# Weight tiles times q and k in f16 parts, exponentials read from PSUM, four counted groups per query block

## The reference, cut to what matters

```python
xr = jnp.einsum('nd,rdf->rnf', x, W)          # graph attention, per edge type r
qi = xr[etype, dst] @ q;  kj = xr[etype, src] @ k
alpha = leaky_relu(qi + kj, 0.2)              # softmax of alpha over the edges of each dst
out = segment_sum(a * xr[etype, src], dst) + b
...
qf, kf = phi(q), phi(k)                       # linear attention, phi(x) = x+1 if x>0 else exp(x)
y = (qf @ (kf^T v)) / max(qf . sum(kf), 1e-6);  y @ W_out + b_out
```

## Time and profile before

| | |
|---|---|
| runs, us | 1745.96, 1751.33, 1743.84 (median 1745.96) |
| profiled execution, its own time | 1746.55 us |
| its span, first to last instruction | 1744.8 us |
| PE, PEld busy | 1631.8 us (94%), 1191.5 us (68%) |
| DVE, ACT, POOL busy | 1308.5 us (75%), 774.8 us (44%), 138.1 us (8%) |
| mean granted TensorE clock | 0.962 |
| DMA | 183.3 MB, 105 GB/s over the span |

### The profile page before, as it was taken

One profiled execution on the slowest core, in us unless ns is written; L12 is line 12 of the kernel. 1 busy time (PEld: TensorE's weight loads), 2 busy tenths in 40 slices (PEclk: granted clock), 3 DMA queues, 4 the chain that ended last, 5 costly groups with the idle time before them and its releaser, 6 DMA issues.

```text
span 1744.8 us, 34402 instructions
## 1 busy us (share of the span) xinstructions
PE 1631.8 (94%) x10547; PEld 1191.5 (68%) x10548; DVE 1308.5 (75%) x2631; ACT 774.8 (44%) x1021; POOL 138.1 (8%) x245
## 2 busy tenths in 40 slices
PE   4999999999999999879999999989899799999987
PEld 3566667778755666479999999986555455555544
DVE  8699876786649999258899898972764377777785
ACT  4331112331234565168888898862212133333342
POOL 2000000000000000000000000000000033333340
PEclk9999998987999999989999999989999999999998
DMA  5111123224467664541004132132664631011122
GB/s 192 38 57 61 60 59 116 78 88 143 156 186 221 197 201 141 152 126 58 30 30 133 46 111 73 40 99 85 196 182 138 199 139 54 1 53 54 60 62 89
DMA packets 130308, 183.30 MB, mean 105 GB/s; under 512 B 14934, under 2 KB 100088, under 8 KB 130220
## 3 DMA queue, kind: packets, MB, share of 16 engines
q1 hardware_dynamic: 130220, 182.17, 33.5%
HBM read 121.33 MB, written 60.81 MB: 104 GB/s over the span
## 4 chain that ended last, share of the span: by engine, by line
PE 80%; DVE 8%; issue 4%; DMA 3%; ACT 2%; DVEq 1%; POOL 1%; SPq 1%; ACTq 0%; POOLq 0%
PE ps L2041 22%; PE ps L1992 12%; PE ps L2099 7%; PE ps L2098 7%; PE ps L1819 6%; PE ps L1806 4%; PE ps L1807 4%; PE ps L1808 4%; PE ps L1901 3%; PE ps L1880 3%; PE ps L2110 1%; PE ps L1977 1%; DVE oh_q L1340 1%; DMA xr_d<-ev 1%; PE ps L1862 1%
## 5 line engine op out<-in xcount | busy, mean ns | idle before, releaser
L2041 PE MATMUL ps<-xrh,pf 128*128 (+1 forms) x2400 | 399.4, 329 | 11.3 <-DVE pf L1617 11.3
L2041 PEld LDWEIGHTS ps<-xrh,pf 128*128 128x128 f32 x2400 | 393.1, 191 | 17.7 <-issue 15.3
L1806 PE MATMUL ps<-w_hi,xt_hi 128*128 128x384 f16 x600 | 198.8, 331 | 23.1 <-DVE ev L1663 14.7
L1613 DVE SCALAR_TENSOR_TENSOR vb<-vb,tb 128x1260 f32<-128x1260 f32 x120 | 172.8, 1465 | 53.1 <-ACT vb L1114 52.2
L1340 DVE TENSOR_SCALAR oh_q<-pat,codeT,neg_w 125x630 f16<-125x630 uint16 x420 | 186.4, 444 | 34.3 <-PE ps L1819 23.5
L2098 PE MATMUL ps<-x,ph 128*128 (+1 forms) x600 | 196.6, 328 | 15.8 <-POOL pl L916 9.9
L1617 DVE SCALAR_TENSOR_TENSOR pf<-vb,CT 128x1260 f32<-128x1260 f32 x120 | 175.7, 1467 | 34.9 <-PE ps L2041 34.9
L1807 PE MATMUL ps<-w_lo,xt_hi 128*128 128x384 f16 x600 | 198.9, 332 | 0.0
L1808 PE MATMUL ps<-w_hi,xt_lo 128*128 128x384 f16 x600 | 198.7, 331 | 0.0
L2099 PE MATMUL ps<-x,ph 128*128 (+1 forms) x600 | 197.8, 330 | 0.0
L1114 ACT ACTIVATE vb<-qbc,kcol 128x1260 f32<-128x1260 f32 x120 | 161.0, 1345 | 39.1 <-DVE pf L1617 37.7
(11 more groups left out here) (235 smaller groups left out, 2454.9 us busy)
## 6 DMA issues: line engine op xcount, KB each, us to landing
qbc<-tq_d SPq DMA_DIRECT2D x12, 1260.0 KB, 6.4
wst<-in_L_gnn_W SPq DMA_DIRECT2D x60, 192.0 KB, 3.2
xr_d<-ev SPq DMA_DIRECT2D x60, 192.0 KB, 2.0
xrh<-xr_d SPq DMA_DIRECT2D x4, 2880.0 KB, 14.9
x_d<-ev SPq DMA_DIRECT2D x60, 192.0 KB, 2.3
mb_d<-mb SPq DMA_DIRECT2D x30, 310.1 KB
mb<-mb_d SPq DMA_DIRECT2D x30, 310.1 KB
x<-x_d SPq DMA_DIRECT2D x2, 3840.0 KB, 19.3
```

The costliest lines, as they stand in the source:

```text
L1613: dve.scalar_tensor_tensor(vb[j][:, :], vb[j][:, :], 2.0, tb[j][:, :], ALU.min, ALU.max).then_inc(v_step, 1)
L1806: pe.matmul(ps[:, bank, 0:CW], a_hi, hi[:, k, :], start=(k == 0), stop=False)
L2041: mm = pe.matmul(out[b], pf[j][:, b * DB:b * DB + P], x, start=(first and b % 2 == 0), stop=False, skip_group_check=True)
```

## The change

- `wq_tile`: ACT writes f16 hi parts of each weight tile (times 16, `wt_high`), DVE the lo parts (`wt_low`), POOL those of q and k, and PE does 18 f16 matmuls for a tile in place of 6 in f32. A tile stands ahead of each step of a block, from the third step of the first block on; tiles 34 and 35 stand in the attention rows.
- A query block has four windows (`QW = 4`), and the attention rows keep three.
- ACT reads the query products straight from PSUM (Relu with the bias folded in), and DVE makes `QF` from PSUM in one instruction; the banks are now freed by that (`q_out`; `q_free` is gone). DVE's lo part of chunk 5 moves behind the first block.
- `bsum` and `acc_d<-X` are gone: the two biases enter the output projection as a matmul of three bf16 rows per product (20 of them), and its input rows are read from `x`.
- Layer 1's `node_columns` moves into the attention rows (blocks 5 to 9), `wqk_hi` and `wqk_lo` into blocks 2 and 3.
- In keys and values DVE reads the window's registers ahead of its waits.
- Layer 2: hi and lo parts of chunks 2 to 5 are made in thirds between the pairs of the chunk before; the first weights of the aggregation start before the last pair.

```diff
+            def wt_high(t):
+
+                act.wait_ge(wt_in[t % 6], 16 * (t // 6 + 1))
+                if t >= 3:
+                    act.wait_ge(wt_used, t - 2)
+                act.activation(wt_hi[t % 3][:, :], wt[t % 6][:, :], ACT.Copy, scale=SPLIT).then_inc(wt_hi_done, 1)
+
+            act.wait_ge(bq_done, 1)
             for c in range(2):
                 for fb in range(3):
-                    wa = W_Q + 3 * (3 * c + fb)
-                    late_out(wa)
-                    late_out(wa + 1)
+                    q = 3 * c + fb
+                    wa = W_Q + QW * q
+                    for k in range(K6):
+                        if k in (2, 4, 5)[:QW - 1]:
+                            late_out(wa + (2, 4, 5).index(k))
+                        wt_high(6 * q + k)
                     for g in range(NRG):
-                        n = (3 * c + fb) * NRG + g
-                        act.wait_ge(q_free, n + 5)
-                        act.wait_ge(q_out, n + 1)
-                        act.activation(q_m[g % 2][:, :], q_t[g % 2][:, :], ACT.Relu, scale=-1.0).then_inc(q_mm, 1)
+                        n = q * NRG + g
+                        act.wait_ge(q_done, n + 1)
+                        if n >= NRG:
+                            act.wait_ge(q_out, n - NRG + 1)
+                        act.activation(q_m[g][:, :], ps[:, g, 0:RG], ACT.Relu, bias=nbq[:, q:q + 1], scale=-1.0).then_inc(q_mm, 1)
                         act.wait_ge(q_mm, n + 1)
-                        act.activation(q_m[g % 2][:, :], q_m[g % 2][:, :], ACT.Exp, scale=-1.0).then_inc(q_ee, 1)
-                    late_out(wa + 2)
+                        act.activation(q_m[g][:, :], q_m[g][:, :], ACT.Exp, scale=-1.0).then_inc(q_ee, 1)
+                    late_out(wa + QW - 1)
                 w_hi_part(C_O + c)
...
+                if 1 <= m < 2 * R - 1:
+                    with act.Fori(0, 3) as ii:
+                        x2_hi(m, ii)
+                        act.wait_ge(w_in[c % 2], 16 * loads_to(c))
+                        weights_free(act, c - 2)
+                        act.activation(w_hi[c % 2][:, ds(2 * ii, 2), :], wst[c % 2][:, ds(2 * ii, 2), :], ACT.Copy).then_inc(w_hi_done, 1)
...
-                        count_part(W_K + 2 * ii + j + 1)
+                        one_hots(W_K + 2 * ii + j + 1, *of_w)
...
+            def wt_low(t, k):
+
+                dve.wait_ge(wt_hi_done, t + 1)
+                dve.scalar_tensor_tensor(wt_lo[k % 3][:, :], wt[k][:, :], SPLIT, wt_hi[k % 3][:, :], ALU.mult, ALU.subtract).then_inc(wt_lo_done, 1)
+
+            def query_block(q):
+
+                wa = W_Q + QW * q
+                for k in range(K6):
+                    wt_low(6 * q + k, k)
+                    if k in (1, 3, 4)[:QW - 1]:
+                        count_part(wa + (1, 3, 4).index(k) + 1)
+                for g in range(NRG):
+                    n = q * NRG + g
+                    dve.wait_ge(q_ee, n + 1)
+                    dve.scalar_tensor_tensor(sub(QF, q)[:, g * RG:(g + 1) * RG], ps[:, g, 0:RG], sub(bq1, q), q_m[g][:, :],
+                                             ALU.add, ALU.max).then_inc(q_out, 1)
+                count_part(wa + QW)
+
             count_part(W_Q)
             dve.wait_ge(ct_out[0], 16 * (3 * NB // 2 + 2) + 16)
             dve.wait_ge(ct_out[1], 16 * (3 * NB // 2 + 1) + 16)
-            for c in range(2):
-                if c == 1:
-                    dve.wait_ge(xb_done, 1)
-                with dve.Fori(0, 3) as fb:
-                    for u in range(2):
-                        count_part(W_Q + 3 * (3 * c + fb) + u + 1)
-                    for g in range(NRG):
-                        n = (3 * c + fb) * NRG + g
-                        dve.wait_ge(q_done, n + 1)
-                        dve.wait_ge(q_out, n + 1)
-                        dve.tensor_scalar(q_t[g % 2][:, :], ps[:, g, 0:RG], sub(bq_col, 3 * c + fb), None, ALU.add).then_inc(q_free, 1)
-                        if g % 2:
-                            for g2 in (g - 1, g):
-                                n2 = (3 * c + fb) * NRG + g2
-                                dve.wait_ge(q_ee, n2 + 1)
-                                dve.scalar_tensor_tensor(sub(QF, 3 * c + fb)[:, g2 * RG:(g2 + 1) * RG], q_t[g2 % 2][:, :], 0.0, q_m[g2 % 2][:, :],
-                                                         ALU.max, ALU.add).then_inc(q_out, 1)
-                    count_part(W_Q + 3 * (3 * c + fb) + 3)
-                    if c == 1:
-                        for u in range(3):
-                            dve.tensor_tensor(sub(X, 3 * fb + u), sub(X, 3 * fb + u), bsum[:, :], ALU.add).then_inc(xb_done, 1)
-            dve.tensor_tensor(X[:, NB - 1, :], X[:, NB - 1, :], bsum[:, :], ALU.add).then_inc(xb_done, 1)
+            dve.wait_ge(bq_done, 1)
+            query_block(0)
+            w_lo_part(5)
+            with dve.Fori(1, K6) as q:
+                query_block(q)
...
+                        x2_lo(m, ii)
+                        if 1 <= m < 2 * R - 1 and i0 == 1:
+                            low_piece(c, ii - 1)
...
+                    cols = slice(k * P, (k + 1) * P)
+                    pe.matmul(o, hi[:, cols], q_hi, start=(t % (WT_TILES // 2) == 0 and k == 0), stop=False, skip_group_check=True)
+                    pe.matmul(o, hi[:, cols], q_lo, start=False, stop=False, skip_group_check=True)
+                    last = pe.matmul(o, lo[:, cols], q_hi, start=False, stop=(nb == K6 - 1), skip_group_check=True)
...
-                    wa = W_Q + 3 * (3 * c + fb)
-                    of_w = [window(pe, wa + u)[1:] for u in range(3)]
+                    wa = W_Q + QW * (3 * c + fb)
+                    of_w = [window(pe, wa + u)[1:] for u in range(QW)]
                     for k in range(K6):
-                        if k in (2, 4):
-                            count_window(wa + k // 2 - 1, 6, *of_w[k // 2 - 1])
+                        if k in (2, 4, 5)[:QW - 1]:
+                            u = (2, 4, 5).index(k)
+                            count_window(wa + u, 6, *of_w[u])
+                        t = 6 * (3 * c + fb) + k - 2
+                        if t == 0:
+                            pe.wait_ge(kvd_done, 2)
+                            pe.wait_ge(qk_ready, 70)
+                        if t >= 0:
+                            wq_tile(t)
                         w_h, w_l = w_hi[cc % 2][:, k, fb * P:(fb + 1) * P], w_lo[cc % 2][:, k, fb * P:(fb + 1) * P]
                         for step, (w, t) in enumerate(((w_h, xt_hi), (w_h, xt_lo), (w_l, xt_hi))):
                             for g in range(NRG):
                                 n = (3 * c + fb) * NRG + g
-                                if k == 0 and step == 0:
-                                    pe.wait_ge(q_free, n + 1)
+                                if k == 0 and step == 0 and n >= NRG:
+                                    pe.wait_ge(q_out, n - NRG + 1)
                                 last = pe.matmul(ps[:, g, 0:RG], w, t[:, k, g * RG:(g + 1) * RG], start=(k == 0 and step == 0),
                                                  stop=(k == K6 - 1 and step == 2))
                                 if k == K6 - 1 and step == 2:
                                     last.then_inc(q_done, 1)
-                    if c == 0 and fb == 0:
-                        pe.wait_ge(kvd_done, 2)
-                        pe.wait_ge(qkn_in, 64)
-                    for t in range(3 * (3 * c + fb), 3 * (3 * c + fb) + 3):
-                        wq_tile(t)
-                    count_window(wa + 2, 6, *of_w[2])
-
-            of_w = window(pe, W_A - 1)[1:]
-            for t in range(WT_TILES // 2, WT_TILES // 2 + 3):
-                wq_tile(t)
-            count_window(W_A - 1, 6, *of_w)
...
+                if i < 2:
+                    wq_tile(WT_TILES - 2 + i)
+                if i >= NB // 2:
+                    if i == NB // 2:
+                        pe.wait_ge(wqk_step, 4)
+                    node_columns(wqk_hi, wqk_lo, 2 * R * H, 2 * i - NB, 2 * i - NB + 2)
...
+                    if c < C_X and q % PM == 0:
+                        pe.matmul(ps[:, 6 + n % 2, 0:CW], one3[:, :], orow[:, (c - C_O) * CW:(c - C_O + 1) * CW], start=True, stop=False)
...
-            pe.wait_ge(wqk_step, 4)
-            node_columns(wqk_hi, wqk_lo, 2 * R * H)
```

More of the change, by code:

```diff
@@ L157, in build @@
         yt_lo = place("yt_lo", [P, K6, NPAD], F16, 159984 + 15360)
[L158 to L159 removed]
+        q_m = [place(f"q_m{j}", [P, RG], F32, 70656 + 1280 * j) for j in range(NRG)]
         kvd = place("kvd", [P, K6, AW], F32, 134144)
@@ L905, in _, with p_low @@
                 pool.memset(pl2[j][:, GW:GW + 4], 0.0).then_inc(one_done, 1)
+            def p_low(g, r, ss):
+                for j in range(2):
+                    n = H * R * NB + (g * R + r) * NB + 2 * ss + j
+                    pool.wait_ge(phi_done, n - U2 + 1)
+                    pool.wait_ge(mm_done, n + 1)
```

(46 more changed lines are left out.)

316 lines of the change are left out of this document (188 added, 128 removed).

## The result

The changed kernel took 1727.07 us, the median of four runs (1723.63 to 1733.05), beside 1747.02 for the kernel before: a ratio of 0.989, 95% interval 0.986 to 0.992. It is faster by 1.1%, some 20 us where 28.5 were forecast, and the time lies in the range of 1703 to 1735. The profiled execution is the slowest of the four, with a span of 1731.3 us.

The account below looks back on a forecast made before the run. PE set the pace before, partly at its lower clock; DVE would bound the changed query blocks at 22.4 us. Gains 0.2 + 15.4 + 4.6 - 1.0 + 1.0 + 8.3 = 28.5 took 1746.55 to 1718 us, range 1703 to 1735.

Parts of the forecast that it names:

- Keys and values: Key-value stage: DVE's register reads ahead of the wait save a gap, gain 1 us (0 to 2.6), an estimate.
- Query stage: Query blocks: 22.4 us each, stage as long as before with more work in it, gain 0.2 us (-8 to +9).
- DVE becomes the bound, by 2 us: Query blocks: DVE needs 22.4 us per block against 20.2 us for PE at full clock.
- Attention rows: First normalisation to first projection matmul: 49.8 us after 65.2, gain 15.4 us (9 to 18).
- rival (a): Query blocks and attention rows: clock stays low in the new order, +10 and +5 us, total 1733; chance 0.15.
- Output projection: Projection stage: moved `node_columns` gain 4.6 us, bias matmuls lose 1.0 us (0 to 3.3).
- 14 of the 20 fall where DVE's maxima set the pace, so 6 count: loss 1.0: Output projection: bias matmuls at 0.163 us each, only 6 of 20 cost time, loss 1.0 us (0 to 3.3).
- Layer-2 products: Layer 2: weight parts made in thirds cut stalls, new loss 11.7 of the old 20, gain 8.3 us (4 to 12).
- Rival (b): Layer-2 products: stalls only change place, DVE's longer turn taking the split's gain, +7 us, total 1725; chance 0.12.
- Rival (c): Query blocks: PE and DVE in lockstep over one set of one-hot tiles, 29.4 us a block, +42, total 1760; chance 0.06.
- rival (d): Query tiles: small matmuls keep the old pace of 0.109 us, 2.0 us a tile, +41, total 1759; chance 0.03.
- (e): DVE's lo part runs faster and attention turns take 4.3 us, total 1706; chance 0.04.

Follow-up runs that it names:

- the first experiment: Changed kernel with PE's four window-word reads put ahead of the last window of the block before: 1720.66 us, ratio 0.985 to the kernel before the change.

## Why the prediction was right, and where it was off

- **Keys and values**, -1.0 forecast: the query stage starts at 249.3 after 250.0, -0.7.
- **Query stage**: first normalisation forecast at 400.0, or 399.0 with the gain in the keys and values, measured 402.9. The step that failed is "DVE becomes the bound, by 2 us". I summed PE as 20.2 us of matmuls and left the four register reads out, though the prediction prices such a read on DVE at 0.55 us. PE needs 20.2 + 2.05 + 0.3 to 1.7, the most of it where the clock is lower behind the stop, so 22.5 to 24, and passes DVE's 22.2. From the end of the first block's `QF` to that of the sixth it took 119.2 us where the prediction's terms give 114.5, 4.7 more; what lies before and behind was 1.8 shorter than summed. That the earlier trace rows show no such stop has its reason in the same trace, in a row that the prediction did not read:

```profile
L448 PEldq TENSOR_LOAD <-tabrow x3: 295/298/308, 319.0 to 320.4; - x3
```

Three words were read beside the window of 319.24 us, which took 3.37 at the lower clock. The price was to be had there: four reads at 0.7 us are longer than a window of 1.91 us. DVE's own sum was good, 22.15 in the first experiment. The lo part took 0.95 us, at the top of its bounds.
- **Attention rows**: forecast 49.8 us, measured 455.3 - 402.9 = 52.4. Turns with windows gave 6.0 (forecast 6.1), but the first turn ran at the lower clock and took 5.8 where 4.0 were forecast. Turns without gave 4.47 at full clock, a little under my 4.6, but two of the six ran at the lower clock at 5.9. The tail took 4.9 of its 6. In the first experiment, where none of the six ran low, the stretch took 48.6. It was the clock's part, rival (a), that I had set aside. What PE did before the clock fell in one execution and not in another of the same code stays open.
- **Output projection**: `node_columns` -4.6 forecast; from the first projection matmul to the second product it is 5.4 us after 9.7, -4.3. The bias matmuls were the other step that failed, "14 of the 20 fall where DVE's maxima set the pace, so 6 count: loss 1.0". Measured +4.4, from the second product to the steady end of the stage (222.4 us after 218.0). The unit price was 0.35 and not 0.163, and PE, not DVE, paced the part in which most of them fall: 18 times 0.35 are 6.3, and the only wait for DVE there shrank from 2.4 to 0.8 us.
- **Layer-2 products**: -8.3 forecast, -9.0 measured, and 9 (by the ratios) to 11 (by the medians) by undoing that part alone. Rival (b) falls. The stop ahead of chunk 5 stayed, as forecast (7.2 us behind a store).
- **Sum**: +2.7 (the 0.7 of the keys and values in it) - 12.8 - 4.3 + 4.4 - 9.0 = -19.0, against the medians' 20. The 9.5 us that are missing from the forecast are 3.9 up to the first normalisation, 2.6 in the attention rows, 3.4 of bias matmuls and 0.3 of `node_columns`, less 0.7 in layer 2. Rival (c) did not come as a whole; rival (d) falls, at 0.46 us a tile; so does (e), with a lo part of 0.95 us. The bounds of the terms, as they stand, add up to 1700 and 1740, not to 1697 and 1749; the stated range is inside both. That the query stage, with the wrong engine as its bound, was out by only 2.9 us is luck: PE with its stops came out at 22.5 to 24 us a block, close to DVE's 22.4.
- **Not shown**: no run puts back the f32 tiles, the old way to `QF` or `node_columns` alone. What they gave is read from the stages, and only the layer-2 part, the fourth window, the early reads and the rows of the bias were each tried by themselves.
- The rule that a load of 128 columns takes 107 ns (the Trainium skill, "TensorE: Matmul & The Clock Gate", "LDWEIGHTS (loading the stationary operand)") is near the duration of one record here, 0.09 to 0.10 us, for 3 rows as for 128. It set no pace for the tiles, where starts lie 25 ns apart. It showed only where a load could not run beside a matmul, at the bias.

## What to carry to other kernels

Sum an engine's queue as well as its work: register reads, at 0.7 us a word here, cost nothing while the queue is ahead, and all of it where the instruction before them waits for another engine. When two engines come out within 10% of each other, as PE and DVE here, the bound may be the ring of their handovers; test it by halving one engine's work before moving anything. Give a small matmul among large ones as many rows as its neighbours, zeros if need be: 0.2 us each here.

## What the hardware showed that was not expected

- In the bias matmuls a weight load of 3 rows does not run beside a matmul of 128 rows, nor a full load beside the small matmul: 0.35 us for a bias matmul of 384 columns, 0.15 with zeros added up to 128 rows.
- POOL keeps DVE out. A one-hot of 0.25 us that starts with POOL's subtraction of 1.64 us takes 1.67 us. The Trainium skill ("SBUF — State Buffer", on who interferes with whom) calls the port pair that the two share an exclusive lock held for the whole instruction, and the pair of rows at 328.57 and 328.58 agrees: the one lasts as long as the other. POOL's product in place does not agree: while that of 330.29 us runs (2.30 us), the one-hot of 331.61 takes its usual 0.24.
- Four reads of a register word from SBUF take 2.7 us of PE's queue, 0.30 us each for the read and the rest for the arithmetic on it and the gaps between.
